# Four row scatters of a unit, issued as one burst or as four steps among other work

## The reference

```python
k = _causal_dwconv(hidden @ Wk.T, ckw, ckb)          # and v, q likewise
for c0 in range(0, S, CHUNK):                        # CHUNK = 128
    g = _grad_fn(W_state, k[:, sl], v[:, sl]) * GRAD_SCALE
    (S_state, W_state), Wtraj = jax.lax.scan(step, (S_state, W_state), xs)
    ...
out = retrieved @ Wo.T
out = out * jax.lax.rsqrt(jnp.mean(out * out, -1, keepdims=True) + EPS) * norm_g
x = _layernorm(x + out * (hidden @ gW.T + gb))
scores = jnp.einsum('bsh,eh->bse', x, gate_w)
chosen = jnp.argmax(scores, axis=-1)                 # one of 8 experts
x = _layernorm(x + (x + expert_w[chosen] @ x))
```

## Time and profile before

| | |
|---|---|
| median of 3 runs | 544.11 us |
| lowest and highest | 542.71 and 547.35 us |
| span of the profiled execution | 578.0 us |
| PE busy | 458.5 us (79%) |
| DVE busy | 376.7 us (65%) |
| POOL busy | 326.8 us (57%) |
| ACT busy | 309.7 us (54%) |
| POOL, the 64 scatters (L1033) | 68.7 us busy |

### The profile page before, as it was taken

How to read it: one execution, slowest core, us unless ns; L and a number is a source line. 1 busy time by engine, 2 the same in 40 slices (tenths; PEclk the granted TensorE clock), 3 DMA queues, 4 the chain that set the end, 5 groups by cost and what they waited for, 6 DMA issues and landing times.

```text
span 578.0 us, 11149 instructions
## 1 busy us (share of the span) xinstructions
PE 458.5 (79%) x3502; PEld 347.1 (60%) x3502; DVE 376.7 (65%) x1123; ACT 309.7 (54%) x779; POOL 326.8 (57%) x451
## 2 busy tenths in 40 slices
PE   4589889999888998888998898766858774855773
PEld 2356656777665877667675775555646553644662
DVE  3365886898795868769789696777644543333433
ACT  1254375566575485665738656464656553314544
POOL 2004535446748686685757657672477666445466
PEclk9797999999998999998999999885887987768788
DMA  8412352345553536445263545474364644425431
GB/s 228 130 74 61 107 124 71 120 129 101 158 130 96 161 85 164 95 141 135 79 176 74 157 110 151 134 231 110 93 178 133 177 140 137 131 91 161 130 120 43
DMA packets 61354, 73.21 MB, mean 127 GB/s; under 512 B 17293, under 2 KB 48206, under 8 KB 61296
## 3 DMA queue, kind: packets, MB, share of 16 engines
q1 hardware_dynamic: 50624, 46.12, 28.5%
q0 software_dynamic: 8848, 25.44, 16.6%
q10 hardware_dynamic: 1824, 0.93, 0.6%
HBM read 44.19 MB, written 19.22 MB: 110 GB/s over the span
## 4 chain that ended last, share of the span: by engine, by line
PE 41%; DVE 20%; ACT 11%; issue 10%; POOL 8%; another core or an unknown queue 5%; DMA 3%; SPq 1%; ACTq 0%; POOLq 0%; DVEq 0%
DVE kq_in L559 8%; PE bank L518 6%; PE bank L1248 5%; PE bank L605 4%; POOL sorted_rows L1033 3%; PE bank L536 3%; ACT rows L966 2%; PE bank L920 2%; PE both L1248 2%; ACT os L1282 2%; PE bank L686 2%; DVE gt L609 1%; PE both L886 1%; PE bank L1225 1%
## 5 line engine op out<-in xcount | busy, mean ns | idle before, releaser
L1287 POOL DMA_INDIRECT out<-os,xs_token x71 | 70.1, 988 | 46.0 <-ACT os L1282 26.4
L1033 POOL DMA_INDIRECT sorted_rows<-rows,index x64 | 68.7, 1074 | 30.0 <-issue 16.6
L1248 PE MATMUL bank<-shared,front 128*128 x212 | 60.6, 435 | 27.3 <-ACT rs L1267 8.5
L518 PE MATMUL bank<-front 128*64 128x256 f32 x512 | 64.8, 408 | 13.3 <-DMA bias_t<-in_bias_t 7.7
L559 DVE SCALAR_TENSOR_TENSOR kq_in<-shared,conv_w,kq_in 128x256 f32<-128x256 f32 x144 | 69.0, 536 | 9.5 <-ACT kq_in L553 9.3
L605 PE MATMUL bank<-front 128*128 128x256 f32 x256 | 63.1, 396 | 4.8 <-DVE bias_g L324 4.8
L1248 PEld LDWEIGHTS bank<-shared,front 128*128 128x128 f32 x212 | 43.9, 219 | 36.5 <-issue 30.3
L518 PEld LDWEIGHTS bank<-front 128*64 128x64 f32 x512 | 38.8, 148 | 34.4 <-issue 10.8
L605 PEld LDWEIGHTS bank<-front 128*128 128x128 f32 x256 | 48.2, 196 | 12.7 <-issue 6.6
L937 DVE SCALAR_TENSOR_TENSOR y<-bank,rms,gt 128x256 f32<-128x256 f32 x64 | 26.5, 476 | 17.1 <-POOL rms L933 10.2
L1252 DVE BATCH_NORM_STATS2 st<-bank 128x6 f32<-128x256 f32 x53 | 20.2, 421 | 26.3 <-remote 11.9
(11 more groups left out here) (212 smaller groups left out, 1185.3 us busy)
## 6 DMA issues: line engine op xcount, KB each, us to landing
front<-sorted_rows SPq DMA_DIRECT2D x71, 130.0 KB
front<-in_hidden_t SPq DMA_DIRECT2D x16, 512.0 KB
decay<-gate_clear SPq DMA_DIRECT2D x16, 512.0 KB
y<-in_hidden POOLq DMA_DIRECT2D x16, 512.0 KB
q<-kq_in SPq DMA_DIRECT2D x64, 64.0 KB, 2.1
carry<-carry_rows SPq DMA_DIRECT2D x32, 128.0 KB, 2.8
hq<-hq SPq DMA_DIRECT2D x64, 64.0 KB
shared<-in_w_expert SPq DMA_DIRECT2D x2, 1024.0 KB
```

Source lines behind the costliest of these rows:

```text
L518: ins = pe.matmul(halves[half(side), kind, :, :], w[:, k, kind * D:(kind + 1) * D], pairs[:, k, side, :, :], start=k == 0, stop=k == KH - 1)
L1033: pool.indirect_dma_start(sorted_rows[:, :], bass.IndirectOffsetOnAxis(index[i2][:, b:b + 1], 0), R[:, b, :], None, bounds_check=NE * REGI ...
L1248: ins = pe.matmul(both[:, i, :], xs_t[t % TURNED][:, i, k, :], w_expert[:, k, bass.ds(expert, 1), :], start=k == 0, stop=k == KH - 1)
L1287: pool.indirect_dma_start(out[:, :], bass.IndirectOffsetOnAxis(xs_token[t % LOADS][:, i:i + 1], 0), os_[o][:, i, :], None, bounds_check=TO ...
```

## The change

The `yield` after the loop over the four scatters moves into the loop: each scatter ends a step. `ORDER` gets three more mentions of each epilogue. With these taken out, the new `ORDER` is the old one word for word; each unit's second, third and fourth scatter stands three other steps behind the one before it. The wait at L963 is written as a function and has the same value as before. No wait stands between the scatters. Lines behind 910 move by four (L1033 becomes L1037, L955 becomes L959).

```diff
+    def scattered_before(c, g):
+
+        return 16 + (c * (G // 2) + g // 2) * NB * 16
+
     def epilogue(c, g):
...
-        act.wait_ge(s_scatter[i2], c * (2 * NB * 16) + (g // 2) * NB * 16 + 16)
+        act.wait_ge(s_scatter[i2], scattered_before(c, g))
...
         for b in range(NB):
             pool.indirect_dma_start(sorted_rows[:, :], bass.IndirectOffsetOnAxis(index[i2][:, b:b + 1], 0), R[:, b, :], None,
                                     bounds_check=NE * REGION - 1, oob_is_err=False).then_inc(s_scatter[i2], 16)
-        yield
+            yield
...
-    "l4r3e2r2p5e1l4r3e2l4s5s5l4l4s5e1r3p6e2p6p6l4e2p6r3p6l4p6p6e0l5p7e1s4s5p6p6l5e1r4l5l5e2s6r3e1l5r2r4e1l5l5e3s5r4p7e2s6s6p7"
+    "l4r3e2r2p5e1l4r3e2l4s5s5l4l4s5e1r3p6e2p6p6l4e2p6r3p6l4p6p6e0l5p7e1e0s4s5p6e0p6l5e1e0r4l5l5e2s6r3e1l5r2r4e1l5l5e3s5r4p7e2"
```

More of the change, by code:

```diff
@@ L1313 @@
     "l2e0p4l2p4p4p4r1p4l3s2r2p4p4e0l3s3l3e0s3e1p6l3e1r1e0l3s4s3r2s4l3r2l3s4e1l3l3l4e1p5s3p5s4p5s4e0p5p5l3p5p5r1r2s4l4l4p5p5p5"
-    "l4r3e2r2p5e1l4r3e2l4s5s5l4l4s5e1r3p6e2p6p6l4e2p6r3p6l4p6p6e0l5p7e1s4s5p6p6l5e1r4l5l5e2s6r3e1l5r2r4e1l5l5e3s5r4p7e2s6s6p7"
-    "e3l5p7e3p7p7l5e3p7r4p7e1l6p6e1e1l5e2s5p7e2p7s5p7e1e2e2e1l6e2l6r5l6e4r4e3l6r3p7l6p8r5s6e3l6s7e4p8e2l6s7p8s7e4l6p8s6r5p8s6"
-    "pbe2p8e4p8p8pal6e3l7p8e2p8e2l7r6s7e3s6r5l7l7e3e3p9p8r5e5e4s7s8e3r4e5r6l7l7s8l7p9e3e3l7e4p9p9l7e5p9l8r6e3l7p9p9p9p9e5s7l8"
@@ L1317 @@
[L1317 to L1324, removed]
@@ L1325 @@
-    "eex0x0efx0x0x0eex0x0x0m0efeex0x0efm0efefx0efefx0efx0m0x0x0x0x0x0x0x0z0x0z0x0efx0x0x0x0x0x0x0x0x0x0x0x0x0x0x0x0x0z0z0z0z0"
-    "z0x0z0x0x0x0x0x0x0x0x0x0x0x0x0x0x0x0x0x0x0x0x0x0x0x0x0x0x0x0x0x0x0x0x0x0x0x0x0x0x0x0x0x0x0x0x0x0x0x0x0x0x0x0x0x0x0x0x0x0"
-    "x0x0x0x0x0x0x0x0x0x0x0x0x0x0x0x0x0x0x0x0x0"
+    "l4r3e2r2p5e1l4r3e2l4s5s5l4l4s5e1r3p6e2p6p6l4e2p6r3p6l4p6p6e0l5p7e1e0s4s5p6e0p6l5e1e0r4l5l5e2s6r3e1l5r2r4e1l5l5e3s5r4p7e2"
+    "s6s6p7e3l5p7e3p7p7l5e3p7r4p7e1l6p6e1e1l5e2s5p7e2p7s5p7e1e2e2e1l6e2l6e1r5l6e4e1r4e3l6e1r3p7l6p8r5s6e3l6s7e4p8e2l6s7p8s7e4"
@@ new lines @@
+    "l6p8s6r5p8s6pbe2p8e4p8p8pal6e3l7p8e2p8e2l7r6s7e2e3s6r5e2l7l7e3e2e3p9p8r5e5e4s7s8e3r4e5r6l7l7s8l7p9e3e3l7e4p9p9l7e5p9l8r6"
+    "e3l7p9p9p9p9e5s7l8p9l8p9l8e3e4s8r7e3r6e4l8e3l8e4r6e3e4e5s7e6p9l8r5r7e6s9e4e5e4pas8pas9e6pas8l8r7pae4pal8pal8e6pae5l9pae4"
+    "pal9e5l9s8s8r7e5e5e4l9e6r8e4s9pcs9e4l9e7r7e4r6l9sar8e6pbl9pbpbe7sae7l9e5l9s9s9r8e7pbpbl9pbs9pbe6lae5r8e6pbe5pbe6e5pae5e7"
+    "e6pbe5e6lalae5r9lasbe5r8e6lalae8e7pbr7sasae8r9e6lasbpce8pclapcsalar9pcpcpcpclbsae7pce7pdsbr8lbe7e8lblae6sae7e6pce7sbe6r9"
@@ new lines @@
+    "rae7e6lbr9e8e6pflbscrasce9e9sce8rae7sbsclbpdpcsbpdlbpde9pdralbpdpde9pde8pdlblce8lbpdpde7sblclce7pee8rbe7lce8rae7r9pde9e7"
+    "lclceae8scsdldlcrbsde9e8sdpeeaeapepelce8rbpelcsdscpesdpepee9rbealde8e9e8ldrclde8sde9e9e8eapepee8lde9ebldebrbealde9selde9"
+    "pfrcpfebebeasepfldseeae9e9rceapfe9eaebpfe9eapfpfe9rcseraececrdw0leeaebpfleeaecpfeaecealeleseeaebrdleealeebpeeasfseleeble"
+    "ebebebebrbrdpfebebeclfrdeby0edpfeby0lfsfeby0y0y0lelfecedsfy0reedlfw0sfecx0lfrereececlfecrex0x0eeedw0edsfsfx0lfx0eeedx0ec"
@@ new lines @@
+    "lfx0y0eex0eeecx0eclfx0x0x0x0x0ecx0x0x0x0ecx0x0x0ecrfeex0ecx0x0edecrfedx0rfx0edededrfedededx0edx0efx0edefx0x0edx0x0eeedx0"
+    "efefx0x0x0x0x0x0x0x0x0eex0x0x0x0x0x0efeem0x0x0x0x0x0eex0m0eex0x0x0efx0eex0m0m0x0x0eeeex0x0efx0x0x0eex0x0x0m0efeex0x0efee"
+    "m0efefeex0efefeex0efx0m0x0x0x0x0x0x0x0z0x0z0x0efx0x0x0efx0x0x0efx0x0x0efx0x0x0x0x0x0x0x0z0z0z0z0z0x0z0x0x0x0x0x0x0x0x0x0"
+    "x0x0x0x0x0x0x0x0x0x0x0x0x0x0x0x0x0x0x0x0x0x0x0x0x0x0x0x0x0x0x0x0x0x0x0x0x0x0x0x0x0x0x0x0x0x0x0x0x0x0x0x0x0x0x0x0x0x0x0x0"
@@ L1328 @@
+    "x0x0x0x0x0x0x0x0x0"
 )
```

## The result

The changed kernel takes 557.20 us in the median of 4 runs (555.80 to 557.69), against 544.11 before: 13.1 us more, ratio 1.0215, 95% interval 1.0148 to 1.0282 (the quotient of the two medians, 1.0241, lies inside it). Some executions of one and the same kernel are over 1.5% longer than its fastest; the ratios leave these out, but a profile can be of one. Slower was forecast, but less than half as much: 548.9 us, and 557.2 lies beyond the range's upper end of 553.5. The profiled execution of the change spans 555.8 us.

A forecast was written before the change was run, and what follows sets the result against it. Waits between engines bound the kernel; 2.0 + 1.1 + 1.7 + 1.6 + 0.3 - 1.6 = 5.1 us, less 0.3 for issue, gave 544.11 + 4.8 = 548.9 us. Own range 546 to 551.5; 8-in-10 range 540.5 to 553.5.

The forecast's parts named there:

- landings hold the norms: At ACT's norms two units later: later last scatters land later and delay norms, partly passed on; 548.9 us, chance 0.55.
- The landing, 3.06 us: Each unit's last scatter was taken to land 3.06 us after it starts, from the one row at unit 4.
- the sign that the prediction named against itself: The forecast is wrong if the last scatter, standing alone, lands in clearly less than 3 us.
- The rival of quicker landings: Scatters spread apart land 2.0 us after their start; sum +0.4 us, 544.5 us, chance 0.12.
- the sum by it, +2.5 us: With the skill page's estimated 2.3 us landing, norms of units 8, 10, 11 each 0.76 us less late: 546.6 us.
- The length of what was hoisted: On POOL, the rstd block takes 1.83 us, moving the last scatter by +1.9 us, or +2.1 with the halo copy.
- What a wait behind the norm takes up: ACT's idle time behind the norms of units 8 and 9 absorbs 0.65 and 0.80 us, leaving +1.1 and +0.3.
- the slack of unit 5: Unit 5's landing at 279.7 precedes the norm of unit 7 at 279.97, ACT being late anyway: 0.
- Unit 0's gain: At unit 0 ck comes 2.6 us earlier on POOL; PE being busy, -1.6 us was counted.
- Units 1, 11, 12, 15: All priced at 0: unit 1 bound 1.3 us late, unit 11 bound -1.1, unit 15's last scatter 5.1 us later.
- All of it counts: Rival: every delay at units 1, 4, 6 to 9 counts, no unit 0 gain; +10.6 us, 554.7 us, chance 0.14.
- Hidden: Rival: waits behind the norms absorb their lateness, leaving unit 4's 2.0 against unit 0's 1.6; 544.5 us, chance 0.11.
- faster: Rival: ck at unit 0 gains 2.6 us, unit 11's block 1.1, late scatters cost nothing; 540.4 us, chance 0.08.

The follow-up runs named there:

- four_after: The change's order with four rows and index buffers and four scatter semaphores instead of two, against the kernel before: ratio 1.0033.
- before_again: The kernel before, unchanged, profiled and timed once more: ratio 0.9995 to the kernel before.
- block_4_5, 6_8 and 9: Burst order of the kernel before, rstd block hoisted ahead of scatters only in units 4 and 5, 6 to 8, or 9: ratios 1.0156, 1.0141, 1.0116.
- spread_0_3: Only the scatter bursts of units 0 to 3 spread, the others as in the kernel before: ratio 0.9981.
- spread_10_15: Only the scatter bursts of units 10 to 15 spread, the others as in the kernel before: ratio 1.0018.
- front_0_9: The change for units 0 to 9 with scatters put back ahead of the rstd block, bursts from unit 10, against the kernel before: ratio 1.0000.
- the test: Small GpSimd instructions run behind the end of the kernel before, alone and beside VectorE: 0.16 us each alone, eight took 4.89 us beside scans.

## Why the prediction was right in kind and wrong in size

**That landings hold the norms: right.** It named ACT's idle time ahead of the norms of units 6, 8, 10 and 11, ended by the landing; it stands there, and ahead of those of units 7 and 9 too. four_after shows that it is the cause.

**The landing, 3.06 us: near, a little long.** In the change the last scatters of units 4 to 9 landed 2.67, 2.68, 2.60, 2.58, 3.10 and 3.17 us after they began (start of the norm less start of the scatter), 2.80 in the mean. At units 6 and 7, where the last scatter stands alone behind the block, it is 2.60 and 2.58: less than 3, the sign that the prediction named against itself, but by far too little to carry the time down. The rival of quicker landings (2.0 us) falls. The Trainium skill's figure for the gpsimd path (DMA: Bandwidth & Descriptors, anatomy of one DMA), an estimated 2.3 us, is below all six, though four of them (2.58 to 2.68) lie no further from it than from 3.06; the sum by it, +2.5 us, is further from what came than the one by the row. (That sum leaves units 4 and 7 as they are. With 2.3 us there too, as the rival of quicker landings does it, it would be +1.5.)

**The length of what was hoisted: this step failed.** "The rstd block takes 252.43 to 254.26, 1.83 us [...] the last scatter moves by +1.9 us where the block alone is hoisted". I took one duration, that of one block behind its burst, and carried it to six places to which blocks were moved. At unit 4 DVE runs its scans there. (The figures do not quite follow either: 1.83 less 0.1 of issue is 1.7, not 1.9; the 0.1 is taken off later for units 6, 8 and 9 only, and at unit 9 the 0.17 us of issue was already in. This is 0.3 us a unit at most.) The distance from first to last scatter's start, and what follows if it and the measured landing are put into the prediction's own formula (first scatter before + distance + landing - norm before):

| unit | before | after | shift | forecast shift | norm late by formula | forecast |
|---|---|---|---|---|---|---|
| 4 | 4.68 | 8.43 | 3.75 | 2.0 | 3.3 | 2.0 |
| 5 | 4.05 | 7.85 | 3.80 | 1.9 | 1.3 | 0 |
| 6 | 4.48 | 7.65 | 3.17 | 1.8 | 2.5 | 1.1 |
| 7 | 4.20 | 6.79 | 2.59 | 2.1 | 1.2 | 0.3 |
| 8 | 4.20 | 6.35 | 2.15 | 1.8 | 2.1 | 1.7 |
| 9 | 4.09 | 7.94 | 3.85 | 3.1 | 2.3 | 1.6 |

The formula with measured lengths gives 12.7 us where the forecast had 6.7 less 0.3, and 12.1 were measured in the stretch. With before_again's times as the kernel before it is 13.6 to 11.7, so the match is good to some 2 us, no better. With 12.7 in place of its own terms the forecast would have been 544.11 + 12.7 - 1.6 = 555.2. Three things lengthened the distance: small instructions beside DVE (1.8 us more at unit 4, 1.4 at unit 6), 0.54 to 0.55 us of issue behind a short last instruction instead of 0.17 (units 4, 5, 7), and scatters that themselves came to lie beside DVE's scans. These are the second and third scatter of unit 5, 1.50 and 1.92 us instead of 1.05 and 0.99:

```profile
274.17 1.50 POOL L1037 DMA_INDIRECT sorted_rows<-rows,index  x1 [0.55 <-issue]
275.98 1.92 POOL L1037 DMA_INDIRECT sorted_rows<-rows,index  x1 [0.31 <-issue]
```

The first and the third are one error: moving work changes what it runs beside. The second is an issue gap taken from a single row. At unit 9 the profile of before had already shown a long block, 3.40 us ("one of its instructions took over 2 us"); I priced it in a rival only.

**What a wait behind the norm takes up: not settled.** The 0.65 and 0.80 us of ACT's idle time behind the norms of units 8 and 9 and the slack of unit 5 were taken off. The table without anything taken off fits the measurement (12.7 to 12.1); with 1.4 us off it would be 11.3. The two can't be told apart by one execution each, and the intervals of block_4_5, 6_8 and 9 are too wide for it.

**Unit 0's gain: seen there, open at the end.** k_n waited 2.29 us instead of 5.01 for ck, the 2.7 us forecast as 2.6:

```profile
147.82 0.38 ACT L647 ACTIVATE k_n<-bank 128x256 f32<-128x256 f32 x1 [2.29 <-POOL ck L715]
```

From the norm of unit 1 to that of unit 2 the six profiles with unit 0 spread need 22.2 to 22.9 us, those with its burst 24.0 to 26.1, so some 2 us arrive there. Further on it blurs: to the norm of unit 4 the change needed 70.7 us and before 74.6, but spread_0_3, with the early units spread, 74.8, and spread_10_15, with bursts, 71.5. spread_0_3 and front_0_9, which have the early spreading and not the loss, are at 0.998 and 1.000, and both intervals hold -1.6 us as well as nothing. Whether it was a term of the end time stays open.

**Units 1, 11, 12, 15: put at 0, and nothing contradicts it** beyond 1% (spread_0_3, spread_10_15). The norm of unit 3 did wait for a landing, 2.99 us. The last scatter of unit 15 came 5.1 us later after its first, as forecast, and cost nothing that shows.

**The rivals.** "All of it counts", 554.7, came nearest, with chance 0.14: it had the stretch at unit 9 and took off nothing, but kept 1.9 us for the block. Hidden, quicker and faster fall. The range's upper end should have held a block that meets DVE in every unit, not in one: the 1.1 us that it added at unit 9 for that, in units 4 to 8 as well, would have made 10.6 + 5 x 1.1 = 16.1 us, and 557.2 would have lain inside.

So the chain of cause is shown by runs (block, then landing), and the lengths by the traces and the test. Two things are not shown. No run hoists the block to a place where DVE is quiet, so how much of the loss is the lengthening and how much the hoist itself is worked out from the table, not measured. And how much of the end's 13.1 us comes through a lower granted clock: PE was busy 5.2 us longer in the stretch, and between the norms of units 6 and 7 and of 7 and 8 the clock was 0.88 and 0.94 in the change, 0.93 and 1.00 before, but it varies as much between executions of one order.
